# A cross-attention and RWKV block on one core: the beginning reordered, and the key and query stacks stored and loaded in other pieces

## The chip, the core and the metric

The kernel runs on one core of a Trainium2 chip. Its engines are TensorE (PE), VectorE (DVE), ScalarE (ACT), GpSimd (POOL) and SyncE (SP), which here only issues DMAs. The metric is the time of one execution on the device in microseconds; several runs give a median, and one further execution was profiled.

## The reference

Eight sequences (B = 8) of 256 tokens with 256 channels attend to a context of 1601 rows each, and the result goes through a second block.

```python
q, k, v = x @ Wq + bq, ctx @ Wk + bk, ctx @ Wv + bv      # 32 query heads, 8 key heads, 8 digits each
scores  = einsum('bkgld,bksd->bkgls', q, k) / sqrt(8) + mask
x = layernorm(softmax(scores) @ v @ Wo + bo + x) * gamma + beta
# second block, channels in 32 heads of 8, with a state of 8 x 8 per head:
xk, xw, xv, xr, xg = token-shift mixes of layernorm(x)
s = k v^T + w * s;  out = r (u k v^T + s)                # scan over the 256 tokens
x = x + (groupnorm(out) * silu(g)) @ Wo.T;  then a gated feed-forward
```

## The kernel before, in words

The program is written out by hand for five engines, with semaphores between them. It is a pipeline over turns (`it`, 0 to 9). In turn `it` element b = it is scored and weighed, a = it + 1 is split and stacked, f = it + 2 is projected, c = it - 1 goes through the output projection and the second block's scan, and d = it - 2 through its feed-forward. A turn has 52 steps; in each TensorE scores two tiles, ScalarE exponentiates them, TensorE weighs the values with them, and the other work is put between at fixed steps.

**Precision by parts.** Keys and queries are float32 values split into three bf16 parts (high, middle, low), and the products of the parts that matter are added within one matmul by stacking them: 6 pairs of parts (`Q_PARTS`, `K_PARTS`) x 8 digits = 48 partitions (`DOT`), for two key heads at partitions 0 to 47 and 64 to 111. So each element has stacks `k_stack[g]`, `q_stack[g]` for g = 0, 1, each with four key heads. Partitions 32 to 63 and 96 to 127 are first cleared (lines 1495, 1496): 1.0 for keys, 0 for queries. Three partitions above the 48 take the row shift.

**From parts to stacks.** The parts leave SBUF for DRAM and return as stacks. `store_k_parts` (line 321) writes each of the six key slots (parts 0, 0, 0, 1, 1, 2) as a DMA of its own (64 partitions x 1601 bf16) into `k_stacked`, laid out as [element, key head, slot, digit, 1601]. `store_q_parts` (line 326) writes six slots x two channel halves, 12 DMAs, into `q_stacked` [element, head, slot, digit, 256]. `load_stacks` (line 332) waits for both and reads a stack by two DMAs for keys (48 partitions x 2 heads x 1601) and two for queries (48 x 8 heads x 256). All of them are SP's, in SP's program order, in every turn: stack 1 of b at step 0, right ahead of the residual rows `x_rows` of c (line 359), both stores of a at step 8, the spread of the values (line 364) at step 18, the next context at step 20, stack 0 of a at step 26.

**POOL's order in a turn** (line 577 on): copy the values, add `bo` to `x_rows` once they have landed (`add_bo`, 528), split queries and keys of a (`split_q`, `split_k`, 507, 496), then the roots for the layer norms of c (`root`, 520). VectorE's layer norm (1359 to 1373) waits for the root, and VectorE's row maxima of stack 1 (`reduce_step`) stand behind it.

**The beginning** runs once. SP loads w_kv, b_kv, w_q, chan and ident (456 to 460, one semaphore `early_in` for all five), the context in four pieces and x_t. VectorE clears both stack pairs and a few borders and `vs` (1493 to 1499). TensorE waits for `early_in` and `cleared`, writes a product of zeros over the accumulator `po`, then projects (`first_projection`, 1053): four pieces of keys and values into banks 7, 5, 7, 5, each reuse waiting for ScalarE's bias, and the queries into bank 6. ScalarE (`project`, 628) adds the bias and makes the high and middle parts, VectorE (1314 to 1323) the rests and low parts, each over all 1601 keys. SP loads the mask, waits for the parts, stores 6 + 12, loads stack 0. VectorE looks at the mask (`see_mask`) while it waits. Then four rounds on the first 128 keys give the row maxima, the shift is turned, split, sent through DRAM onto the stack (`shift_to_dram`, `shift_to_stack`), and turn 0 begins. SP loads the context of element 1 only after `mask_seen`, because the mask lies in the context's buffer. POOL issues 46 late loads of weights (line 617) once the last piece of the context is there.

```python
for r, n in enumerate(K_PARTS):                                                    # 323
    sp.dma_start(k_st_d[a % B][:, r], k_parts[:, n, :]).then_inc(k_out.sem, 16)
sp.dma_start(k_stack[g][p0:p0 + DOT, :, :],                                        # 340
             k_st_d[n % B][k0:k0 + 2].rearrange("k r d s -> (r d) k s"))
```

## Time and profile before

| What | Before |
|---|---|
| median of 3 runs | 1243.32 us (1239.51 to 1243.42) |
| the profiled execution, its own time | 1244.15 us |
| its span, first to last instruction | 1242.3 us |
| mean granted TensorE clock | 0.942 |
| busy: PE, DVE, ACT, POOL | 85%, 50%, 70%, 25% |
| first context piece issued, last | 3.18 us, 4.7 us |
| first score tile of turn 0 | 76.35 us |
| DMA written to DRAM, read | 18.62 MB, 50.74 MB |

A DMA row of a view gives the mean busy share of the core's 16 DMA engines in tenths, slice by slice, and the row under it GB/s. A timeline row may hold several instructions of one kind (x8); its length is from the first's start to the last's end. In square brackets stands how long the engine was idle before, and what released it. The profile names buffers without their numbers. All matmuls stand under line 710, a helper's.

### The profile page before, as it was taken

To read this page: it belongs to the slowest core of one execution; us is meant where nothing else is said; L and a number is where in the kernel's file an instruction comes from. 1 tells how busy PE (TensorE), PEld (TensorE's weight loads), DVE (VectorE), ACT (ScalarE), POOL (GpSimd) and SP (SyncE) were. 2 spreads that over 40 slices of the span, in tenths; PEclk is the share of its full clock that TensorE was granted. 3 is DMA by queue.
4 is the path that set the end of the run, shared out by engine and by line. 5 is a ranking of instruction groups with operands and counts; after the bars stand their busy time and mean duration, and the time that the engine had idled before them with its cause. 6 is when DMAs were issued, how large, how long until landed. Compare 5 with 4: busy or idle time off the path is not lost.

```text
span 1242.3 us, 18191 instructions
## 1 busy us (share of the span) xinstructions
PE 1050.1 (85%) x7100; PEld 374.4 (30%) x7100; DVE 615.0 (50%) x1113; ACT 870.0 (70%) x953; POOL 305.6 (25%) x349
## 2 busy tenths in 40 slices
PE   3058998899999998999999999999998899986663
PEld 1012222232334233333333233323332233313312
DVE  5324122575375645484367536564547334735463
ACT  1037988688877887778877887888777877884010
POOL 6204104140232305230414023220523001401140
PEclk9569999999999999999999999999999899999766
DMA  5643413271227123441337122803252022300310
GB/s 174 160 96 120 95 55 66 55 151 55 42 75 142 24 75 94 63 103 55 74 65 141 55 46 72 149 16 88 82 69 35 2 42 31 57 1 1 51 26 11
DMA packets 65565, 87.47 MB, mean 70 GB/s; under 512 B 8208, under 2 KB 48192, under 8 KB 65472
## 3 DMA queue, kind: packets, MB, share of 16 engines
q1 hardware_dynamic: 63536, 82.91, 31.2%
q0 software_dynamic: 1936, 3.32, 0.9%
q8 instruction: 58, 0.95, 0.3%
q14 instruction: 35, 0.29, 0.1%
HBM read 50.74 MB, written 18.62 MB: 56 GB/s over the span
## 4 chain that ended last, share of the span: by engine, by line
PE 35%; issue 20%; DVE 14%; ACT 13%; POOL 8%; DMA 6%; SPq 3%; POOLq 0%; DVEq 0%; ACTq 0%
PE psum L710 35%; ACT probs L649 10%; DMA vs<-v_c 5%; DVE row_max L1162 3%; DVE vs L1282 2%; SPq L371 2%; POOL k_rest L501 1%; POOL k_parts L505 1%; DVE vs L1275 1%; POOL xm L536 1%; DVE k_stack L1495 1%; POOL vs L553 1%; ACT L649 1%; ACT L686 1%; DVE xa L1249 1%
## 5 line engine op out<-in xcount | busy, mean ns | idle before, releaser
L649 ACT ACTIVATE probs<-psum 128x1024 f32<-128x1024 f32 (+1 forms) x832 | 800.5, 1022 | 244.5 <-PE psum L710 243.5
L710 PE MATMUL psum<-probs,v_aug 128*9 128x512 f32 (+1 forms) x3328 | 423.8, 608 | 0.1
L710 PE MATMUL psum<-q_stack,k_stack 64*128 64x512 bf16 (+1 forms) x1664 | 291.5, 391 | 54.4 <-ACT probs L649 43.3
L710 PEld LDWEIGHTS psum<-q_stack,k_stack 64*128 64x128 bf16 (+1 forms) x1664 | 71.2, 95 | 425.6 <-ACT probs L649 350.4
L1282 DVE TENSOR_TENSOR_SCAN vs<-w_c,vs 128x514 f32<-128x514 f32 x64 | 101.8, 1591 | 21.7 <-POOL vs L544 19.9
L710 PEld LDWEIGHTS psum<-probs,v_aug 128*9 128x9 f32 (+1 forms) x3328 | 62.1, 90 | 161.9 <-issue 148.1
L553 POOL TENSOR_TENSOR vs<-r_c,vs 128x512 f32<-128x512 f32 x64 | 86.1, 1354 | 100.3 <-DVE tmp L1421 59.6
L1162 DVE TENSOR_REDUCE row_max<-psum 128x8 f32<-128x1024 f32 x64 | 78.0, 1219 | 46.3 <-PE psum L710 45.8
L536 POOL TENSOR_TENSOR xm<-tmp,xa 128x512 f32<-128x512 f32 x40 | 45.6, 1156 | 206.3 <-DVE tmp L1269 206.3
L523 POOL TENSOR_TENSOR rstd<-moments,eps 128x2 f32<-128x2 f32 x24 | 4.7, 194 | 302.4 <-DVE moments L1235 302.4
L1209 DVE COPY o_raw<-psum 128x512 f32<-128x512 f32 x32 | 22.1, 692 | 98.6 <-PE psum L710 98.6
L710 PE MATMUL psum<-k_stack,q_stack 48*128 48x128 bf16 x512 | 26.8, 225 | 48.2 <-DMA q_stack<-q_stacked 29.5
L1269 DVE SCALAR_TENSOR_TENSOR tmp<-psum,chan,sx 128x256 f32<-128x256 f32 x80 | 33.4, 473 | 49.8 <-PE psum L710 49.8
L710 PE MATMUL psum<-ctx_t,w_kv 128*128 128x400 f32 (+1 forms) x128 | 49.5, 521 | 6.7 <-DVE attn L1223 6.0
L488 POOL COPY v_aug<-v_st 128x384 f32<-128x384 f32 x16 | 8.1, 505 | 161.7 <-PE psum L710 160.0
L1275 DVE TENSOR_TENSOR vs<-k_c,vs 128x512 f32<-128x512 f32 x64 | 47.0, 735 | 0.3
L710 PEld LDWEIGHTS psum<-k_stack,q_stack 48*128 48x128 bf16 x512 | 18.4, 97 | 65.9 <-issue 54.7
L1140 DVE TENSOR_SCALAR kv<-psum,b_kv 128x400 f32<-128x400 f32 (+1 forms) x28 | 17.6, 630 | 39.4 <-PE psum L710 39.4
L710 PEld LDWEIGHTS psum<-ctx_t,w_kv 128*128 128x128 f32 x128 | 23.0, 192 | 26.2 <-DVE attn L1223 8.5
L1469 DVE RECIPROCAL xm<-xm 128x512 f32<-128x512 f32 x8 | 26.8, 3348 | 7.1 <-ACT xm L686 7.1
L1157 DVE TENSOR_REDUCE mask_max<-ctx_t 128x1 f32<-128x1601 f32 x16 | 28.8, 1810 | 0.0
L1131 DVE TENSOR_SCALAR q<-psum,chan 128x256 f32<-128x256 f32 x16 | 7.0, 480 | 39.4 <-PE psum L710 23.8
(175 smaller groups left out, 1062.7 us busy)
## 6 DMA issues: line engine op xcount, KB each, us to landing
vs<-v_c SPq DMA_DIRECT2D x64, 257.0 KB, 7.4
ctx_t<-in_mask SPq DMA_DIRECT2D x8, 1601.0 KB, 6.5
k_stacked<-k_parts SPq DMA_DIRECT2D x48, 200.1 KB
k_stack<-k_stacked SPq DMA_DIRECT2D x32, 300.2 KB, 6.7
ctx_t<-in_ctx_t SPq DMA_DIRECT2D x24, 400.0 KB, 5.9
q_stacked<-q_parts SPq DMA_DIRECT2D x96, 64.0 KB, 2.0
q_stack<-q_stacked SPq DMA_DIRECT2D x32, 192.0 KB, 7.3
ctx_t<-in_ctx_t SPq DMA_DIRECT2D x8, 401.0 KB, 6.3
```

The costliest lines, as they stand in the source:

```text
L371: sp.dma_start(vs[:, j, :, :].rearrange("p e l -> p (e l)"), src.broadcast_to([16, HD, EC * (L + 1)]))\
L536: nc.gpsimd.tensor_tensor(xm[MIX_ORDER[n]][:, :, :], tmp[n % 2][:, :, :], xa[:, :, 1:L + 1], ALU.add)\
L553: nc.gpsimd.tensor_tensor(vs[:, j, :, 0:L], r_c[:, :, :], vs[:, j, :, 0:L], ALU.mult)\
L649: nc.scalar.activation(probs[turn_step % NP][t][0:w, :, :], ps[t][0:w, :, :], ACT.Exp).then_inc(exped.sem, 1)
L710: return nc.tensor.matmul(dst, lhsT, rhs, start=start, stop=stop)
L1157: nc.vector.tensor_reduce(mask_max[:, a, lc:lc + 1], ctx_t[:, lc, :], AX.X, ALU.max, apply_absolute_value=True).then_inc(mask_seen.sem, 1)
L1162: nc.vector.tensor_reduce(row_max[:, 8 * r:8 * r + 8], psum[:, 6:8, :].rearrange("p a (u k) -> p (a u) k", k=P), AX.X, ALU.max)\
L1209: nc.vector.tensor_copy(o_raw[:, :], po).then_inc(o_kept.sem, 1)
L1269: last = nc.vector.scalar_tensor_tensor(tmp[n % 2][:, e, :], halves(at)[:, e, :], vec(f"s{f}", e), sx[:, e, :], ALU.add, ALU.mult)
L1275: nc.vector.tensor_tensor(vs[:, j, :, 1:L + 1], k_c[:, :, :], vs[:, j, :, 1:L + 1], ALU.mult)\
L1282: nc.vector.tensor_tensor_scan(flat, w_c[:, :, :].rearrange("p e l -> p (e l)"), flat, 0.0, ALU.mult, ALU.add)\
L1469: link(nc.vector.reciprocal(std_o[:, :, :], std_o[:, :, :]))
```

## The change

VectorE clears stack pair 0 and POOL pair 1. The loads of w_q, chan and ident are issued behind the context, with a semaphore of their own. The first projection uses banks 0 to 3, and TensorE waits for the clearing only behind it. The split of element 0's keys goes by halves of 801 and 800, interleaved with the biases, and ScalarE runs one small Exp at the start. ScalarE's queue stores element 0's queries and loads half of its first stack. The mask's load and its look come after the stack loads and after the shift's split. In all turns: keys are stored by three DMAs (the source repeated 3, 2, 1 times) into a layout with the slot outside the key head, queries by six DMAs of the three distinct parts, and a stack is loaded by ten DMAs (each half: two for keys, three for queries) instead of four. POOL's late loads come in another order and behind its clearing. POOL's own waits of the key split (`split_turn`) count without the first turn.

```diff
+RUNS = [(0, 3), (3, 2), (5, 1)]
...
+SPLIT = [(0, 801), (801, 800)]
...
-KV_FIRST = (7, 5, 7, 5)
+KV_FIRST = (0, 1, 2, 3)
...
-        k_st_d = nc.dram_tensor("k_stacked", [B, KV, NR, HD, S], BF16).ap()
-        q_st_d = nc.dram_tensor("q_stacked", [B, NH, NR, HD, L], BF16).ap()
+        k_st_d = nc.dram_tensor("k_stacked", [B, NR, KV, HD, S], BF16).ap()
+        q_st_d = nc.dram_tensor("q_stacked", [B, NH, 3, HD, L], BF16).ap()
...
-        early_in, late_in = sig("early_in", 16 * 5), sig("late_in")
-        cleared, prepared, acc_cleared, v_ones = sig("cleared"), sig("prepared"), sig("acc_cleared"), sig("v_ones")
+        early_in, early_q, late_in = sig("early_in", 16 * 2), sig("early_q", 16 * 3), sig("late_in")
+        cleared, cleared_up = sig("cleared"), sig("cleared_up")
+        prepared, acc_cleared, v_ones, warmed = sig("prepared"), sig("acc_cleared"), sig("v_ones"), sig("warmed")
...
+        k_out, q_out = sig("k_out", 16 * len(RUNS)), sig("q_out", 16 * 3 * EC)
...
+        def split_turn(a):
+            return a - 1 - a // B
+        def load_stack_half(eng, n, g, half):
+            k0, p0 = 4 * g + 2 * half, HALF * half
+            for t in range(2):
+                eng.dma_start(k_stack[g][p0:p0 + DOT, t, :], k_st_d[n % B, :, k0 + t])\
+                  .then_inc(stack_in[g].sem, 16)
+            for r0, m in RUNS:
+                lo, hi = p0 + HD * r0, p0 + HD * (r0 + m)
+                eng.dma_start(q_stack[g][lo:hi, :, :, :].rearrange("p t h l -> p (t h) l"),
+                              q_st_d[n % B][4 * k0:4 * k0 + 8, 0:m].rearrange("h r d l -> (r d) h l"))\
+                  .then_inc(stack_in[g].sem, 16)
+        def store_queries(eng, a):
+            for m in range(3):
+                for c in range(EC):
+                    eng.dma_start(q_st_d[a % B][16 * c:16 * c + 16, m], q_parts[:, m, c, :]).then_inc(q_out.sem, 16)
...
-                for r, n in enumerate(K_PARTS):
-                    sp.dma_start(k_st_d[a % B][:, r], k_parts[:, n, :]).then_inc(k_out.sem, 16)
+                for r0, m in RUNS:
+                    src = k_parts[:, K_PARTS[r0], :].rearrange("p (a s) -> p a s", a=1)
+                    sp.dma_start(k_st_d[a % B, r0:r0 + m].rearrange("r k d s -> (k d) r s"), src.broadcast_to([64, m, S]))\
+                      .then_inc(k_out.sem, 16)
             def store_q_parts(a):
                 sp.wait_ge(q_low.sem, q_low.at(a))
-                for r, n in enumerate(Q_PARTS):
-                    for c in range(EC):
-                        sp.dma_start(q_st_d[a % B][16 * c:16 * c + 16, r], q_parts[:, n, c, :]).then_inc(q_out.sem, 16)
-
-            def load_stacks(n, g):
+                store_queries(sp, a)
+            def load_stacks(n, g, halves=(0, 1)):
                 if n > 0:
                     sp.wait_ge(scored.sem, scored.at(n - 1, TILES // GQ * (g + 1)))
                     sp.wait_ge(sub_reduced[g].sem, sub_reduced[g].at(n - 1))
                 sp.wait_ge(k_out.sem, k_out.at(n))
                 sp.wait_ge(q_out.sem, q_out.at(n))
-                for half in range(2):
-                    k0, p0 = 4 * g + 2 * half, HALF * half
-                    sp.dma_start(k_stack[g][p0:p0 + DOT, :, :],
-                                 k_st_d[n % B][k0:k0 + 2].rearrange("k r d s -> (r d) k s")).then_inc(stack_in[g].sem, 16)
-                    sp.dma_start(q_stack[g][p0:p0 + DOT, :, :, :].rearrange("p t h l -> p (t h) l"),
-                                 q_st_d[n % B][4 * k0:4 * k0 + 8].rearrange("h r d l -> (r d) h l"))\
-                      .then_inc(stack_in[g].sem, 16)
+                for half in halves:
+                    load_stack_half(sp, n, g, half)
...
                 if not general:
-                    load_mask(lo)
+                    sp.dma_start(w_q[:, :, :], dram["L0_xattn_Wq"].rearrange("(c p) n -> p c n", p=P))\
+                      .then_inc(early_q.sem, 16)
+                    sp.dma_start(chan[:, :, :], dram["chan"]).then_inc(early_q.sem, 16)
+                    sp.dma_start(ident[:, :], dram["ident"]).then_inc(early_q.sem, 16)
                     sp.wait_ge(cleared.sem, 1)
+                    sp.wait_ge(cleared_up.sem, 1)
                 store_k_parts(lo)
-                store_q_parts(lo)
-                load_stacks(lo, 0)
+                load_stacks(lo, 0, (0,))
                 if general:
                     full_masks(lo, 0)
+                else:
+                    load_mask(lo)
...
+            pool.wait_ge(v_ones.sem, 1)
+            link(nc.gpsimd.memset(k_stack[1][32:64, :, :], 1.0))
+            link(nc.gpsimd.memset(q_stack[1][32:64, :, :, :], 0.0))
+            link(nc.gpsimd.memset(k_stack[1][96:128, :, :], 1.0))
+            nc.gpsimd.memset(q_stack[1][96:128, :, :, :], 0.0).then_inc(cleared_up.sem, 1)
+            pool.wait_ge(cleared_up.sem, 1)
             pool.wait_ge(ctx_in[NK - 1].sem, ctx_in[NK - 1].at(0))
...
             def project(a):
+                turn = a // B
                 act.wait_ge(early_in.sem, early_in.at(0))
-                for n, (at, w) in enumerate(PIECE):
+                def biased(n):
+                    at, w = PIECE[n]
                     act.wait_ge(kv_proj.sem, kv_proj.at(a, n + 1))
                     nc.scalar.activation(kv32[:, at:at + w], bank(KV_FIRST[n])[:, 0:w], ACT.Identity, bias=b_kv[:, 0:1])\
                       .then_inc(kv_biased.sem, 1)
-                act.wait_ge(kv_biased.sem, kv_biased.at(a))
-                nc.scalar.activation(k_parts[:, 0, :], kv32[0:64, :], ACT.Copy).then_inc(k_high.sem, 1)
+                def high(h):
+                    at, w = SPLIT[h]
+                    act.wait_ge(kv_biased.sem, kv_biased.at(a, 2 * h + 2))
+                    nc.scalar.activation(k_parts[:, 0, at:at + w], kv32[0:64, at:at + w], ACT.Copy).then_inc(first_high.sem, 1)
+                def mid(h):
+                    at, w = SPLIT[h]
+                    act.wait_ge(first_r1.sem, first_r1.at(turn, h + 1))
+                    nc.scalar.activation(k_parts[:, 1, at:at + w], k_rest[:, at:at + w], ACT.Copy).then_inc(first_mid.sem, 1)
+                biased(0)
+                biased(1)
+                high(0)
+                biased(2)
+                mid(0)
+                biased(3)
+                high(1)
+                mid(1)
                 act.wait_ge(q_scaled.sem, q_scaled.at(a))
                 nc.scalar.activation(q_parts[:, 0, :, :], q32[:, :, :], ACT.Copy).then_inc(q_high.sem, 1)
-                act.wait_ge(k_r1.sem, k_r1.at(a))
-                nc.scalar.activation(k_parts[:, 1, :], k_rest[:, :], ACT.Copy).then_inc(k_mid.sem, 1)
                 act.wait_ge(q_r1.sem, q_r1.at(a))
                 nc.scalar.activation(q_parts[:, 1, :, :], q_rest[:, :, :], ACT.Copy).then_inc(q_mid.sem, 1)
+                act.wait_ge(q_low.sem, q_low.at(a))
+                store_queries(act, a)
+                act.wait_ge(cleared.sem, 1)
+                act.wait_ge(k_out.sem, k_out.at(a))
+                act.wait_ge(q_out.sem, q_out.at(a))
+                load_stack_half(act, a, 0, 1)
...
+            nc.scalar.activation(partial_max[:, 0, 0:1], ones[:, :], ACT.Exp).then_inc(warmed.sem, 1)
...
             def first_projection(a, general):
                 for n in range(NK):
-                    if n >= 2:
-                        pe.wait_ge(kv_biased.sem, kv_biased.at(a, n - 1))
                     project_kv(a, n, KV_FIRST[n])
+                pe.wait_ge(early_q.sem, early_q.at(0))
                 project_q(a, 6)
+                if a == 0:
+                    pe.wait_ge(cleared.sem, 1)
+                    zeros = vs[:, 0:2, :, :].rearrange("p j e l -> p (j e l)")
+                    mm(po, zeros[:, 0:P], zeros[:, P:P + 512]).then_inc(acc_cleared.sem, 1)
...
+                def rest(h):
+                    at, w = SPLIT[h]
+                    dve.wait_ge(first_high.sem, first_high.at(lo // B, h + 1))
+                    nc.vector.tensor_tensor(k_rest[:, at:at + w], kv32[0:64, at:at + w], k_parts[:, 0, at:at + w],
+                                            ALU.subtract).then_inc(first_r1.sem, 1)
+                def low(h):
+                    at, w = SPLIT[h]
+                    dve.wait_ge(first_mid.sem, first_mid.at(lo // B, h + 1))
+                    return nc.vector.tensor_tensor(k_parts[:, 2, at:at + w], k_rest[:, at:at + w], k_parts[:, 1, at:at + w],
+                                                   ALU.subtract)
+                rest(0)
+                low(0)
+                rest(1)
                 scale_q(lo, 6)
-                dve.wait_ge(k_high.sem, k_high.at(lo))
-                nc.vector.tensor_tensor(k_rest[:, :], kv32[0:64, :], k_parts[:, 0, :], ALU.subtract).then_inc(k_r1.sem, 1)
+                low(1).then_inc(k_low.sem, 1)
                 dve.wait_ge(q_high.sem, q_high.at(lo))
                 nc.vector.tensor_tensor(q_rest[:, :, :], q32[:, :, :], q_parts[:, 0, :, :], ALU.subtract).then_inc(q_r1.sem, 1)
-                dve.wait_ge(k_mid.sem, k_mid.at(lo))
-                nc.vector.tensor_tensor(k_parts[:, 2, :], k_rest[:, :], k_parts[:, 1, :], ALU.subtract).then_inc(k_low.sem, 1)
                 dve.wait_ge(q_mid.sem, q_mid.at(lo))
                 nc.vector.tensor_tensor(q_parts[:, 2, :, :], q_rest[:, :, :], q_parts[:, 1, :, :], ALU.subtract)\
                   .then_inc(q_low.sem, 1)
                 keep_v(lo, 0, 5)
                 keep_v(lo, 1, 7)
-                if not general:
-                    see_mask(lo, 0)
-                    see_mask(lo, 1)
                 for r in range(4):
                     reduce_step(lo, 0, r, general)
                 negate_shift(lo, 0)
                 split_shift(lo, 0)
+                if not general:
+                    see_mask(lo, 0)
+                    see_mask(lo, 1)
...
-            for g in range(GQ):
-                for p0 in (32, 96):
-                    nc.vector.memset(k_stack[g][p0:p0 + 32, :, :], 1.0)
-                    nc.vector.memset(q_stack[g][p0:p0 + 32, :, :, :], 0.0)
+            for p0 in (32, 96):
+                nc.vector.memset(k_stack[0][p0:p0 + 32, :, :], 1.0)
+                nc.vector.memset(q_stack[0][p0:p0 + 32, :, :, :], 0.0)
```

Moved in `late_loads`: w_o, the rows, maa_w1, the five square weights, Wv and Wg come first, then heads, heads_turned, maa_w2, td_w1 and td_w2; the rest as before. SP's three early loads stand behind `load_x_t` now.

## Rows read from the trace of the kernel before

**Rows 1.** The page: span, granted clock in 40 slices, the mask's reductions.

```profile
span 1242.3 us, 18191 instructions
...
PEclk9569999999999999999999999999999899999766
...
L1157 DVE TENSOR_REDUCE mask_max<-ctx_t 128x1 f32<-128x1601 f32 x16 | 28.8, 1810 | 0.0
```

**Rows 2.** The chain that ended last, first 80 us: start, length (us), what.

```profile
1.46 2.73 DVE k_stack L1495
...
5.96 2.73 DVE k_stack L1495
...
20.07 4.03 PE psum L710 x6
...
35.13 1.83 DVE k_parts L1320
...
50.85 2.03 DMA q_stacked<-q_parts
...
54.32 6.71 DMA q_stack<-q_stacked
...
76.35 0.63 PE psum L710 x2
```

**Rows 3.** Waits of the whole span: us in total, times, longest.

```profile
POOL x_rows L531 <- DMA x_rows<-in_x: 31.2, 7, 5.4
```

**Rows 4.** Timeline of turn 1, by engine: start, length (us), engine, line, operation.

```profile
195.24 0.47 SPq L362 DMA_DIRECT2D x_rows<-in_x  x1
...
202.92 1.27 POOL L531 TENSOR_TENSOR x_rows<-x_rows,rows 128x512 f32<-128x512 f32 x1 [5.43 <-DMA x_rows<-in_x]
...
218.41 0.74 DVE L1242 TENSOR_SCALAR x<-x,moments,rstd 128x256 f32<-128x256 f32 x2 [8.47 <-POOL rstd L526]
...
225.30 0.40 PE L710 MATMUL psum<-k_stack,q_stack 48*128 48x128 bf16 x8 [0.65 <-DVE row_max L1162]
```

**Rows 5.** Timeline of the beginning, and one POOL cast of turn 1.

```profile
11.40 0.80 POOL L617 DMA_DIRECT2D heads<-in_heads  x1 [10.21 <-DMA ctx_t<-in_ctx_t]
...
21.91 3.52 PE L710 MATMUL psum<-ctx_t,w_kv 128*128 128x401 f32 x8
...
25.48 1.08 ACT L632 ACTIVATE kv<-psum,b_kv 128x401 f32<-128x401 f32 x2
...
29.75 1.54 ACT L635 ACTIVATE k_parts<-kv 64x1601 bf16<-64x1601 f32 x1
...
30.93 0.88 DVE L1131 TENSOR_SCALAR q<-psum,chan 128x256 f32<-128x256 f32 x2 [10.97 <-PE psum L710]
...
33.46 0.67 DVE L1318 TENSOR_TENSOR q_rest<-q,q_parts 128x512 f32<-128x512 f32 x1
...
207.85 1.51 POOL L499 CAST k_parts<-kv 64x1601 bf16<-64x1601 f32 x1
```

**Rows 6.** DMA issues from 0 to 14 us: count, KB each, median us to landing.

```profile
ctx_t<-in_ctx_t SPq DMA_DIRECT2D x3, 400.0 KB, 5.9
ctx_t<-in_ctx_t SPq DMA_DIRECT2D x1, 401.0 KB, 4.7
```

**Rows 7.** DMA share (tenths) and rate, 350 to 360 us, 40 slices: key stores.

```profile
DMA  0000000345338555545545545445544469965432
GB/s 0 0 0 0 0 0 0 77 102 102 64 77 270 205 192 192 205 179 179 179 179 192 167 154 167 141 192 192 179 167 192 167 244 376 376 239 159 147 116 103
```

**Rows 8.** The same, 136 to 150 us: the four loads of stack 0.

```profile
DMA  0000092899999998999999920000000000000000
GB/s 0 0 0 0 0 137 55 338 318 123 133 117 147 192 176 171 227 155 105 116 110 129 138 31 10 0 0 0 0 0 0 0 0 0 0 0 0 0 0 0
```

**Rows 9.** Timeline of turn 2: stack 0 issued, stack 0 first read.

```profile
397.97 0.47 SPq L340 DMA_DIRECT2D k_stack<-k_stacked  x1
...
414.02 0.39 PE L710 MATMUL psum<-k_stack,q_stack 48*128 48x128 bf16 x8
```

More of the change, by code:

```diff
@@ L222, in build @@
         mask_seen = sig("mask_seen", LC)
-        stack_in = [sig(f"stack_in{g}", 64) for g in range(GQ)]
+        stack_in = [sig(f"stack_in{g}", 16 * 2 * (2 + len(RUNS))) for g in range(GQ)]
         sub_scored = [sig(f"sub_scored{g}", 4) for g in range(GQ)]
@@ L273, in late_loads @@
             c = dram
-            yield heads[:, :], c["heads"]
-            for m in range(HD):
-                yield heads_turned[16 * m:16 * m + 16, :], c["ident"][0:16, 0:16]
             yield w_o[:, :, :], c["L0_xattn_Wo"].rearrange("(c p) n -> p c n", p=P)
@@ L1499, in _ @@
             nc.vector.memset(vs[:, 0:2, :, :], 0.0).then_inc(cleared.sem, 1)
-            dve.wait_ge(early_in.sem, early_in.at(0))
+            dve.wait_ge(early_q.sem, early_q.at(0))
             all_turns(0, False)
```

25 lines of the change are left out of this document (11 added, 14 removed).

## The prediction

> **What bounds the kernel now.** I read the page first, then the chain that ended last in order of time, the timeline of the first 80 us, the DMA view of three stretches, and the waits. The page gives a span of 1242.3 us; the granted clock stands at 9 tenths or nearly so in the first slice of 31 us, at 5 and 6 in the next two, and at 9 or more through the body of the loop [rows 1]. Ahead of them lies a serial beginning. Its chain [rows 2] runs: VectorE clears the two pairs of stacks from 1.46 on, TensorE starts only at 20.07, the three-way split of the keys ends at 36.96, SP issues 18 stores of which the last begins at 50.85 and has landed at 52.88, four stack loads land by 61.03, four rounds of row maxima and the shift follow, and the first score tile stands at 76.35. Nothing of the loop runs before that, so what the beginning loses in length the whole kernel loses, as long as the loop is untouched. But the change touches the loop too, because the layout of the two DRAM tensors is shared by all turns. There a second chain matters. In each turn POOL waits for the residual rows, which SP issues right behind the four loads of stack 1; seven of eight times it waited, 31.2 us in all [rows 3]. In turn 1 the rows are issued at 195.24, POOL adds the bias at 202.92, runs the two splits behind it in order, and VectorE has idled 8.47 us when the root lets it go at 218.41; TensorE's round at 225.30 waited for VectorE's maximum [rows 4]. So a later landing of these rows lengthens a turn one for one.
>
> **The change, part by part, the beginning.** *Clearing.* The stack blocks cost VectorE 2.73 us each, and with the queries' block and the gaps they start 4.5 apart, four times [rows 2]. Two of the four go to POOL, so VectorE is done at about 11.0 instead of 20.0, and TensorE no longer waits for it before projecting (it waits before its clearing product, behind the queries). POOL's casts give 1.51 us for 1601 elements [rows 5], so about 3 us for 3202 and 1 to 2 for the queries' block, twice: done by 9.5 to 11.5. As an upper bound, a POOL operation with two inputs takes 1.27 for 512 elements [rows 4], which would make it about 22 to 27; SP's first store waits for it, and from 17.5 on it would be the path. I take 11.
>
> *Projection.* It now starts with the first piece of the context. The pieces landed 4.7 and 5.9 us after their issue [rows 6], the first issued at 3.2; three loads (w_q, chan, ident) go behind them, which moves their issue up by 1.5 us, to 1.7. So piece 0 is there at about 6.2 and piece 3 at about 9.3. Eight instructions took 3.52 us, 0.44 each, straight after 20 us of idling [rows 5]; the clock of the first slice, which holds them, is near full [rows 1], so the engine had the 2.4 GHz level after idling from the start, and I take it here too. Four pieces of four make 7.0 us, less a little as the later ones run faster, so the last is done at about 12.6. With four banks TensorE doesn't wait for ScalarE. The table load moves under this wait; the first bias at 25.48 came 1.3 us late for it [rows 5]. At the 1.2 GHz level the four pieces would take up to twice as long, and the projection would end 6 us later.
>
> *Split by halves.* After the last piece: one bias (0.54, half of 1.08), behind ScalarE's middle cast of half 0, then half of a cast (1.54), a subtraction (1.83), a cast and a subtraction [rows 2, 5], with the queries' scaling of 0.88 beside the second cast, 0.1 of it showing. That is 0.5 + 0.5 + 3.4 + 0.1 + 0.3 of handovers = 4.8, so the low part is ready at 17.4 instead of 36.96.
>
> *Stores.* Keys: three issues instead of six. The old ones run at half of the DMA engines: while only they run, the share stands at 4 to 5 tenths and 170 to 205 GB/s [rows 7]. Their DRAM side has an outermost count of 8 (the heads), and the new one has 64 (heads and digits merge), so I expect all 16 engines: 1.2 MB at some 340 GB/s, 3.6 us. Queries: six issues on ScalarE's queue instead of twelve on SP's. Three more steps of some 0.67 bring their low part to 19.6. The first 17 issues of now took 0.82 each (36.96 to 50.85) [rows 2]; at that the sixth begins at 23.7 and has landed 2.03 later, at 25.7. POOL's late loads started at 11.40 [rows 5] and start at the same time now, the big weights first (2.6 MB), so the stores share the engines with them. I add 0.8: both are out at 26.5 (25 to 29), against 52.88.
>
> *Stack loads.* This is the disputed part. Ten loads in place of four, the same bytes: 615 KB of keys and 393 KB of queries. The old ones took 6.5 us with all 16 engines at 9 tenths, the first keys at 318 to 338 GB/s, which would make 1.8 us of keys and leave 4.7 for queries, whose stretches run at 105 to 147 [rows 8]. Their DRAM side begins with a merged count of 48. The new key loads can't merge part and digit, because the heads lie between them: the DRAM side begins with 6. If the outermost count sets the number of engines, as 8 did in [rows 7], six engines carry all keys at 24 GB/s each, 144 together: 4.3 us. The same six also carry 64 query packets each instead of 48 (leading counts 24, 16 and 8 on 12, 16 and 8 engines). If memory limits those packets, the other ten engines have done theirs meanwhile and 2.3 us are left, in all 6.6: 0.1 more than now. If each engine's own rate limits them, 4.7 x 64/48 = 6.3, in all 10.6: 4.1 more. I take 2.0 more, the middle, and call this d. The Trainium skill, DMA: Bandwidth & Descriptors, section "Why a DMA increments its semaphore by 16 and not by 1", says that the outermost counts of both sides set it, by the largest number up to 16 that divides both. By it the key loads run on 6 engines; the share of 5 tenths with a count of 8 agrees. First load: 8.15 from the last store's landing to the last load's [rows 2] becomes 10.15, so the stacks are in at 36.65 against 61.03.
>
> Behind this nothing moves: rounds, shift and its detour take 15.3 as before, 61.03 to 76.35. The mask is loaded behind the stacks, 1.6 MB or some 5 us of transfer, under the rounds. Its two reductions of 1.81 [rows 1] come behind the shift's split, beside the shift's way through DRAM; the next context waits for them, and I set 0.4 for what shows. Gain of the beginning: 24.4 - 0.4 = 24.0.
>
> **The loop.** SP's nine stores fewer and twelve loads more nearly cancel in issue time, and at the stores SP is waiting anyway. Stack 0 is issued at 397.97 and first read at 414.02, 16 us later [rows 9]; 6 more issues and d fit in that. What doesn't fit is the load of stack 1, with the residual rows behind it: they are spread over all engines and land when the slowest is through, so d later. Turns 1 to 6 have the splits on POOL behind this wait and pay 6 x 2.0 = 12; turn 7 has no split and turn 0 no such rows. The sum: 24.0 - 12 = 12.0 less, 1244.15 - 12.0 = 1232.15 on the profiled execution's own time, which stands 0.8 above the median of 1243.32; so 1231 for the median. In general the difference is -26.0 + 7d, one d in the beginning and six in the loop.
>
> **Rivals.** *The engines are all used.* The loads may still spread over 16 engines; then d is 0 and only the beginning changes: 1243.3 - 26.0 = 1217. For it: the destination still has 48 partitions. Against: the key stores at half share, with 64 partitions on their SBUF side. *The loads cost more than they save.* With engine-bound packets, uneven queues or keys below 24 GB/s per engine, d is 4.5: -26.0 + 31.5 = +5.5, 1249. It decides from d = 3.7 on. For it: in [rows 8] the second key load ran at 171 to 227, not at 338, beside query packets. Against: with six engines reading, each meets less traffic. *The beginning gives less.* POOL's clearing or the late loads hold the stores: 5 to 8 us less of it, 1236 to 1239.
>
> **Numbers.** Forecast 0.47, all engines 0.25, less at the beginning 0.10, dearer loads 0.18. Some 0.3% (3.7 us) is what a measurement of this kernel can tell from no change. The forecast's own d runs from 1 to 3, 1224 to 1238, and with a beginning 2 us shorter or longer than reckoned 1222 to 1240. By case: the forecast is faster but for 0.02 within the bound; all engines is faster; of the lesser beginning 0.06 is faster and 0.04 within; of the dearer loads 0.05 is within and 0.13 slower. Faster 0.45 + 0.25 + 0.06 = 0.76, the same 0.11, slower 0.13. The range runs from 1214 to 1247.
>
> **What would show it.** First projection near 6 us, key split ready near 17.4, stacks in near 37, first score near 52. In the DMA view the key stores at 9 tenths, the stack loads at 9 tenths first and then at 3 to 5; POOL's wait for the residual rows at 6.5 us a turn instead of 4.5. It is wrong if the loads keep a share of 9 and take 6.5 us (then nearer 1217), or if POOL's wait passes 8 us (then slower than before), or if the keys' split starts only after 20.

## The result, and the profile after

The changed kernel takes 1247.97 us (median of 20 runs) beside 1243.59 for the kernel before on the same chip (20 runs): a ratio of 1.0033 with a 95% interval of 1.0019 to 1.0047. It is slightly slower, where 1231 and faster was forecast, and lies just outside the forecast's range of 1214 to 1247. One run of each kernel took far longer (1389.71 and 2466.13 us); the ratio goes by the others. Its profiled execution took 1242.88 us, near the low end of its runs (1240.69 upwards), so its rows show some 5 us less than its typical run costs.

The page of the changed kernel, against [rows 1]:

```profile
span 1241.1 us, 18221 instructions
...
PEclk8589998999999999999999999999999999999666
...
L1211 DVE TENSOR_REDUCE mask_max<-ctx_t 128x1 f32<-128x1601 f32 x16 | 28.8, 1810 | 0.0
```

The body is granted 9 tenths as before, so at this resolution the clock doesn't tell the two apart (a small difference in the loop is taken up below), and the mask's two reductions last 1.81 each as before. The chain that ended last, first 64 us (start, length, what), against [rows 2]; L290 are the query stores, L279 and L283 the stack loads:

```profile
5.35 4.54 PE psum L764 x8
...
16.75 0.99 DVE k_parts L1377
...
19.03 0.70 DVE q_parts L1388
19.75 0.63 ACTq L290
...
20.42 2.36 ACTq L290
22.81 2.48 ACTq L290
...
27.63 3.92 DMA q_stacked<-q_parts
...
35.18 12.68 DMA q_stack<-q_stacked
...
48.13 0.62 PE psum L764 x8
...
63.24 0.63 PE psum L764 x2
```

Up to 19.75 everything stands where the forecast had it. Then the last query store lands at 31.55 instead of 26.5, and the stacks are in at 47.86 instead of 36.65: 16.3 us after the stores, where it had been 8.15. The first score stands at 63.24: 13.1 earlier than at 76.35, not 24.

SP's timeline of the same stretch shows what was issued right behind SP's half of the stack loads, while these still ran; the mask is 1.6 MB:

```profile
17.84 3.27 SPq L350 DMA_DIRECT2D k_stacked<-k_parts  x3
31.61 1.71 SPq L279 DMA_DIRECT2D k_stack<-k_stacked  x2
33.36 1.71 SPq L283 DMA_DIRECT2D q_stack<-q_stacked  x3
35.12 0.41 SPq L343 DMA_DIRECT2D ctx_t<-in_mask  x1
```

In the loop, the waits of the whole span (us in total, times, longest), against [rows 3]:

```profile
POOL x_rows L553 <- DMA x_rows<-in_x: 49.6, 7, 7.9
DVE x L1296 <- POOL rstd L548: 42.0, 8, 10.9
```

POOL waits 7.1 us a turn for the residual rows instead of 4.5. What this costs I read from the copy that begins each turn on POOL, v_aug with 65x32; here those of turns 1 and 7:

```profile
181.94 0.21 POOL L514 COPY v_aug<-v_st 65x32 f32<-65x32 f32 x1
...
1001.56 0.21 POOL L514 COPY v_aug<-v_st 65x32 f32<-65x32 f32 x1
```

The six turns between them last 819.6 us. In the kernel before they stood at 197.28 and 1004.01, 806.7. The loop gives back 12.9 of the 13.1. Of the rest, turn 0 is 2.2 shorter (118.7 from the first score to turn 1's copy, where it was 120.9) and what follows turn 7's copy 1.3 longer: the profiled span is 1.2 us below that of the kernel before.

The DMA view (share in tenths and GB/s in 40 slices) of the stack-0 load in turn 0's second half, 121 to 135 us, against [rows 8]:

```profile
DMA  0000022325885233466854445432110000000000
GB/s 0 0 0 0 0 18 37 91 91 164 225 184 84 55 73 109 119 158 184 255 135 167 138 152 146 82 71 60 58 37 25 10 0 0 0 0 0 0 0 0
```

and of the key stores, 341 to 351 us, against [rows 7]:

```profile
DMA  0300000009999999999999999999999993996000
GB/s 0 66 0 0 0 0 0 0 0 231 218 205 192 205 205 205 205 205 205 205 192 205 205 205 205 205 205 205 192 218 205 205 192 107 340 373 226 4 0 0
```

The loads spread thin: shares mostly of 2 to 6, two slices at 8, and a tail at 1 to 3, about 9 us long, where four loads had held 9 tenths for 6.5. The stores did get all engines, as forecast, and moved no faster for it: 6.2 us for 1.2 MB, where 340 GB/s and 3.6 us were reckoned.

### The profile page after: what moved, and what is told of

The parts are those of the page before. It is cut to its first block, busy times and chain, and to the rows that moved or that the text cites. A ratio compares the mean times of both kernels' runs of the same rounds, so it can differ in the third digit from the quotient of the medians.

```text
span 1241.1 us, 18221 instructions
## 1 busy us (share of the span) xinstructions
PE 1051.0 (85%) x7100; PEld 375.7 (30%) x7100; DVE 608.2 (49%) x1111; ACT 870.4 (70%) x956; POOL 314.3 (25%) x353
## 4 chain that ended last, share of the span: by engine, by line
PE 28%; issue 24%; DVE 14%; ACT 12%; POOL 11%; DMA 7%; SPq 2%; ACTq 1%; POOLq 0%; DVEq 0%
PE psum L764 28%; ACT probs L702 9%; DMA vs<-v_c 5%; DVE row_max L1216 3%; DVE vs L1336 2%; SPq L391 2%; POOL k_rest L523 2%; POOL k_parts L527 1%; DVE vs L1329 1%; DMA q_stack<-q_stacked 1%; POOL xm L558 1%; POOL vs L575 1%; POOL rstd L548 1%; POOL k_parts L525 1%; ACT L702 1%
## 5 line engine op out<-in xcount | busy, mean ns | idle before, releaser
L1296 DVE TENSOR_SCALAR x<-x,moments,rstd 128x256 f32<-128x256 f32 x16 | 5.9, 411 | 42.0 <-POOL rstd L548 42.0
```

## The experiments

All are timed in five rounds beside the kernel before, whose median there was 1243.8 to 1245.8. "Wait" is POOL's wait for the residual rows; "six turns" is the time between the two copies above; "stacks" runs from the last query store's landing to the last stack load's. One profiled execution gives each of these.

### Loop: is it the stores and loads, and are they late for the rows?

Four runs. **b_newio** is the kernel before with the change's layouts, stores and loads in all turns, all on SP. **a_oldloop** is the changed kernel with those forms for element 0 alone and the old ones (in DRAM tensors of their own) for elements 1 to 7. **a_xfirst** and **b_xfirst** are the two kernels with SP's order at step 0 turned round:

```
-                            if b is not None:
-                                load_stacks(b, 1)
                             if c is not None:
                                 load_x_rows(c)
+                            if b is not None:
+                                load_stacks(b, 1)
```

> The kernel before, with the new layout, stores (3 + 6) and loads (10 per stack) in all turns, all issued by SP; the beginning is otherwise the old one. If the new loads are what the loop lost, six turns of 2.2 us and the first load a few us longer: 13 to 20 us slower than before, 1257 to 1264, and POOL's wait for the residual rows near 50 us in all. If the loss came with the new beginning instead (clock, phase of the turns), within 3 us of before, and the wait near 31.

> The kernel after, with the new layout, stores and loads for element 0 alone; elements 1 to 7 use tensors of the old layout with the old 18 stores and four loads. Loads theory: the beginning keeps its 13 us and the loop gives nothing back, 1228 to 1234, POOL's wait near 31 us. Rival (the loop lost its time for another reason): 1243 to 1248.

> The kernel after, with SP issuing the residual rows ahead of the loads of stack 1 instead of behind them; the loads stay as they are. If what costs is that the rows queue behind the loads, POOL's wait goes to nearly zero, and the time to 1226 to 1234. If the loads cost in another place (stack 0 late for its rounds, the other DMAs), the wait goes but the time stays above 1240.

> The kernel before with the residual rows first. POOL's wait of 31 us goes; the chain through POOL's splits is the critical one in about every turn by small amounts, so 3 to 10 us faster, 1233 to 1240. If TensorE is just as late by its own work, no change.

| run | median us | ratio [95%] | wait, us | six turns | first score |
|---|---|---|---|---|---|
| before | 1243.59 | | 31.2 | 806.7 | 76.35 |
| after | 1247.97 | 1.0033 [1.0019, 1.0047] | 49.6 | 819.6 | 63.24 |
| b_newio | 1259.63 | 1.0116 [1.0088, 1.0145] | 52.3 | 827.6 | 74.63 |
| a_oldloop | 1227.81 | 0.9881 [0.9853, 0.9908] | 29.9 | 804.7 | 61.96 |
| a_xfirst | 1221.07 | 0.9803 [0.9769, 0.9838] | none | 796.7 | 63.00 |
| b_xfirst | 1237.83 | 0.9936 [0.9910, 0.9961] | none | 796.9 | 76.84 |

The new forms alone make the kernel before 1.2% slower; without them in the loop the change gains 1.2%. With the rows issued first the wait is gone in both kernels and their six turns agree within 0.2 us. So the whole loss of the loop hangs on this one wait: stack 0's loads have 16 us to spare [rows 9], the rows behind stack 1's have none. a_xfirst came out below its range of 1226 to 1234, because the new order takes away not only what the loop had lost but also the wait that the kernel before had (six turns 806.7, then 796.9).

### Loop: six engines, or six more issues?

The rows are issued behind ten loads instead of four. Either the engines are late, or SP is. **b_ten** keeps the old layout and stores of the kernel before, but has ten loads that all begin with a merged count of 48:

```
-  k_stack[g][p0:p0 + DOT, :, :] <- k_st_d[n % B][k0:k0 + 2] "k r d s -> (r d) k s"
+  for t: k_stack[g][p0:p0 + DOT, t, :] <- k_st_d[n % B][k0 + t] "r d s -> (r d) s"
-  q_stack (t h) l <- q_st_d[n % B][4 * k0:4 * k0 + 8] "h r d l -> (r d) h l"
+  the same for heads 0 to 3, 3 to 6 and 6 to 8
```

**b_pad** is b_ten with one row of padding behind each part, so that part and digit can't merge; loads, bytes and stores stay:

```
-        k_st_d = nc.dram_tensor("k_stacked", [B, KV, NR, HD, S], BF16).ap()
+        k_st_d = nc.dram_tensor("k_stacked", [B, KV, NR, HD + 1, S], BF16).ap()
```

**b_newk** and **b_newq** are the kernel before with the change's key or query forms alone. In the expectations below the merged count is given as 96 and a part as sixteen rows. A part has eight rows of digits, so it is 48 rows a load, 48 merged and 6 not, and the padding is a ninth row; 48 is a multiple of 16 too, so what the runs test stays the same.

> The kernel before with its own DRAM layouts and its own 18 stores, but with ten loads per stack in place of four: the keys by t, the queries in three pieces of 3, 3 and 2 heads, so that every load still begins with a count of 96 and can use all 16 engines. Theory of the engines (the loads of the change are late because few engines carry them): the residual rows land as before, POOL's wait for them stays near 31 us (4.5 a turn) or a little over, the time at the kernel before's, 1241 to 1247. Rival, the count of issues (SP issues six more DMAs at about 0.55 us each before the residual rows, so these start 3.3 us later, on whatever engines the loads are): the wait is 48 to 54 us as with the change's loads, and the time 1255 to 1262.

> The run b_ten with one thing more: the keys' DRAM tensor holds a seventeenth row behind each part's sixteen, which is never written or read, so that part and digit no longer merge and each key load begins with a count of 6 instead of 96. Stores, bytes, number of loads and their order are those of b_ten, and so is the rest of the layout. Theory of the engines (it is the outer count that makes the change's key loads late): POOL's wait for the residual rows goes from 28.7 us to 44 to 52, and the time from b_ten's 1240 to 1254 to 1260. Rival (it is the head between part and digit, that is where the rows lie in DRAM, or the three broadcast key stores): the wait stays at 28 to 33 and the time at 1239 to 1243.

> The kernel before with the change's key layout alone: three key stores, and two key loads of 96 rows for each half, which have six as their outer count; six loads per stack in all. Theory of the engines: the keys are 0.6 of a stack's bytes and sit on 6 engines, so most of the lateness is here: POOL's wait 42 to 48 us, time 1250 to 1256. Rival, the count of issues: two issues more per stack, 1.1 us a turn, wait 37 to 40, time 1246 to 1250.

> The kernel before with the change's query layout alone: six query stores, and three query loads for each half on 12, 16 and 8 engines at most; eight loads per stack in all. Theory of the engines: little lateness from the queries alone, wait 33 to 38, time 1243 to 1248. Rival, the count of issues: four issues more per stack, 2.2 us a turn, wait 43 to 47, time 1250 to 1255. The query stores are six instead of twelve, and the last of them is the key stores' predecessor, so the beginning may be some 3 us shorter in both theories.

| run | loads per stack, keys' outer count | median us | ratio [95%] | wait, us | six turns |
|---|---|---|---|---|---|
| b_ten | 10, 48 | 1240.29 | 0.9974 [0.9962, 0.9986] | 28.7 | 803.5 |
| b_pad | 10, 6 | 1257.06 | 1.0094 [1.0071, 1.0117] | 48.2 | 819.2 |
| b_newk | 6, 6 | 1257.26 | 1.0112 [1.0087, 1.0136] | 45.1 | 818.3 |
| b_newq | 8, 48 | 1239.68 | 0.9970 [0.9954, 0.9985] | 33.8 | 807.0 |

Six more issues cost nothing; b_ten is even a little faster than the kernel before. The outer count of the keys alone costs 16.8 us between the medians; the two ran on different chips, and by their ratios to the kernel before it is 1.2%, some 15 us. b_newq's gain is made in the beginning, where six query stores fewer bring its first score to 73.01; its loop is as long as before. SP's timeline and the DMA view of turn 2's stack-1 load, first of b_ten (slices of 0.275 us, 326 to 337):

```profile
326.31 0.79 SPq L341 DMA_DIRECT2D k_stack<-k_stacked  x2
327.15 1.38 SPq L345 DMA_DIRECT2D q_stack<-q_stacked  x3
328.57 0.89 SPq L341 DMA_DIRECT2D k_stack<-k_stacked  x2
329.51 1.39 SPq L345 DMA_DIRECT2D q_stack<-q_stacked  x3
330.95 0.43 SPq L365 DMA_DIRECT2D x_rows<-in_x  x1
```

```profile
DMA  0000759999999998999779999999994000000000
```

and of b_pad, where the loads begin at 332.29 (332 to 343):

```profile
332.29 1.57 SPq L341 DMA_DIRECT2D k_stack<-k_stacked  x2
333.90 1.40 SPq L345 DMA_DIRECT2D q_stack<-q_stacked  x3
335.34 1.48 SPq L341 DMA_DIRECT2D k_stack<-k_stacked  x2
336.86 1.41 SPq L345 DMA_DIRECT2D q_stack<-q_stacked  x3
338.32 0.43 SPq L365 DMA_DIRECT2D x_rows<-in_x  x1
```

```profile
DMA  0000007500368964343344779465989954543110
```

b_ten holds 7 to 9 tenths for 7 us and is through, the rows with it. b_pad swings between 3 and 9 tenths and needs 9 us. Issuing key loads with the small outer count is itself dearer (1.5 us for two instead of 0.8), so the rows are issued 6.0 us after the first load instead of 4.6. Over the seven turns POOL starts on the rows 9.0 us after the first load's issue in b_ten and 11.8 in b_pad; of these 2.8 more, 1.3 lie before the rows' issue and 1.5 behind it. Issue time alone doesn't make the rows late: the kernel before issues them 1.8 us after the first load and b_ten 5.2, and POOL starts at 9.3 and 9.0. The Trainium skill, DMA: Bandwidth & Descriptors, section "Why a DMA increments its semaphore by 16 and not by 1", has a DMA use the largest number of engines up to 16 that divides both outermost counts; a load of 48 rows with 6 outermost on its DRAM side would run on six. The views agree: six of sixteen busy would be 4 tenths at most, and b_pad's share falls to 3 and 4 where b_ten's stays at 7 and more. Which engines carried what was not read out.

The key forms cost more over the runs than in the profile of the changed kernel. Of the profiles shown here and below, the seven that load keys by 6 and have the rows behind them give six turns of 818.3 to 827.6 us, 822.7 in the mean; the six with the rows behind them and keys by 48 give 803.5 to 807.7, mean 805.8. That is 16.9, or 2.8 a turn; the changed kernel's profiled 12.9 is at the low end, which goes with its time at the low end of its runs.

Part of that price lies in the clock. Over the six turns TensorE is granted 0.97 or 0.98 in each of the seven and 0.99 in each of the six, and its matmuls are busy for 751 to 758 us instead of 746 to 749, 6.4 more in the mean, of the 16.9. With the rows first it is 0.99 and 747.5 even with the change's loads (a_xfirst), so the lower clock comes with the wait. How much of the 6.4 adds to the time, and how much lies beside the wait, the runs don't separate.

### The beginning: late loads, mask, queue, keys

Each of these is the changed kernel with one edit. **a_late**: POOL issues its late loads once stack 0 is in. **a_mask**: the mask waits for stack 0. **a_spq**: SP issues the query stores behind the key stores. **a_oldk**: the keys' old layout, six stores and one load per half in all turns. **a_oldkmask**: a_oldk and a_mask.

```
a_late   pool, behind copy_v(lo, 0):  + pool.wait_ge(stack_in[0].sem, stack_in[0].at(0)), then the late loads
a_mask   sp, ahead of load_mask(lo):  + sp.wait_ge(stack_in[0].sem, stack_in[0].at(lo))
a_spq    act: - store_queries(act, a)     sp, behind store_k_parts(lo): + store_q_parts(lo)
a_oldk   k_st_d [B, KV, NR, HD, S]; stores and key loads as in the kernel before
```

> The changed kernel with POOL's 50 or so late loads (3.3 MB) issued only once stack 0 has landed, instead of from 10.85 us on. Theory of the contention (query stores and first stack loads are slow because the late loads fill the same 16 engines): the last query store lands near 27 instead of 31.55, the stack loads take 12 instead of 16.3 from there, and the first score stands at 54 to 58 instead of 63.2; time 1239 to 1243. Rival, the issuing and the few engines alone make it slow: the first score stays at 61 to 64 and the time within 2 us of the changed kernel's 1248.

> The changed kernel with the mask's load (1.6 MB) issued only once stack 0 has landed. Theory that the mask shares engines with the first stack load: the stacks take 13 to 15 us from the last query store instead of 16.3, the first score stands 1 to 3 us earlier, 60 to 62; the time 1244 to 1248, less what the later mask costs the next context's load. Rival, the stacks are limited by the six engines of the keys, which the mask hardly loads more than the others: first score within 0.7 us of 63.2, time unchanged at 1246 to 1250.

> The changed kernel with the six query stores issued by SP behind the key stores instead of by ScalarE. If issuing from ScalarE's queue itself is dear (1.4 us each there), SP issues them at 0.6 to 0.8 from 21 on, they have landed by 28 instead of 31.55, and the first score is 2 to 4 us earlier, time 1244 to 1247. Rival, each issue waits because the engines' queues are full with late loads and key stores, on whatever queue it is issued: SP takes 1.2 to 1.5 us for each too, they land at 31 to 33, and the first score is within 1.5 us of 63.2 or later; time 1247 to 1250.

> The changed kernel with the keys' DRAM layout, six stores and one load per half of the kernel before, everything else of the change kept (queries' new layout, both queues, clearing, halves, banks). Theory of the keys (all that the loop loses is the key loads, whose outer count is 6; the query forms lose nothing): POOL's wait for the residual rows goes back to 32 to 36 us, the six turns to 803 to 808, and the time is 1227 to 1233. In the beginning three more stores of keys cost issue time on SP beside ScalarE's, and the key loads are quicker: the first score at 60 to 64. Rival, the query loads on 12, 16 and 8 engines carry a good part of it once the beginning is short: wait 40 or more, time 1237 or more.

> The run a_oldk with the mask's load issued once stack 0 has landed. Theory that the mask was dear only because its packets stand in line on the six engines that carry the change's keys: with the keys on all engines moving it gives little, the stacks take 7 to 9 us from the last query store instead of 9.1 and the first score stands at 55 to 57 instead of 56.65; time 1222 to 1226. Rival, the mask costs the first stack load by its bytes whatever the keys' engines, as it did with 5.8 us in the changed kernel: stacks in 3.5 to 4, first score at 51 to 53, time 1219 to 1222.

| run | median us | ratio [95%] | first query issue, last landed | stacks, us | first score | wait, us |
|---|---|---|---|---|---|---|
| after | 1247.97 | 1.0033 [1.0019, 1.0047] | 19.75, 31.55 | 16.3 | 63.24 | 49.6 |
| a_late | 1242.04 | 0.9991 [0.9974, 1.0009] | 20.85, 29.2 | 13.0 | 59.12 | 52.3 |
| a_mask | 1241.46 | 0.9981 [0.9962, 1.0000] | 20.94, 31.2 | 10.5 | 56.90 | 50.9 |
| a_spq | 1246.83 | 1.0025 [1.0007, 1.0043] | 20.56, 32.0 | 13.5 | 60.87 | 51.3 |
| a_oldk | 1225.05 | 0.9839 [0.9812, 0.9866] | 19.70, 32.4 | 9.1 | 56.65 | 34.3 |
| a_oldkmask | 1223.40 | 0.9830 [0.9808, 0.9853] | 20.69, 33.2 | 8.3 | 56.67 | 32.2 |

*The mask and the keys.* Moving the mask takes 5.8 us from the stacks and 6.5 from the time, far more than I expected of it. Giving the keys their 16 engines back, with the mask left where it was, takes 7.2. Doing both takes 8.0. So the mask is dear only together with the six-engine keys: with the keys on all engines it costs 0.8. The chain of a_mask:

```profile
27.95 3.25 DMA q_stacked<-q_parts
...
34.64 7.09 DMA q_stack<-q_stacked
...
56.90 0.63 PE psum L765 x2
```

and the DMA view from 31 to 49 us, first of the changed kernel, then of a_mask:

```profile
DMA  0411253535888899999989999999993433422000
```

```profile
DMA  0312533367899794434441000092899999994000
```

In a_mask the stack loads stand without the mask (POOL's last small late loads are issued up to 36.4) and end in slices of 4 tenths; the mask follows behind the gap at 9 tenths. In the changed kernel the mask fills all 16 engines at once and the tail of 3 to 4 tenths comes behind it, at 45 to 48 us. I read that as the few engines that carry the keys having the mask's packets to move too; the 2 x 2 of the runs shows the coupling, the order within an engine's queue was not looked at. a_oldk also came below its range (1225.05, where 1227 to 1233 was expected; first score 56.65 for 60 to 64): I hadn't counted the first stack load's gain.

*The queue.* a_spq's six issues took 20.56 to 28.5, 1.3 us each, like ScalarE's 1.4. So the queue is not what makes them dear, and the rival stands. What does is to be seen in b_newk, whose late loads are all issued by 36.5; its first three query issues, right behind the key stores, are

```profile
40.61 2.01 SPq L333
42.66 1.01 SPq L333
43.72 0.60 SPq L333
```

and all later ones take 0.60. Key stores just issued make the next issues dear, without any late load. a_spq's stacks came 2.8 sooner all the same, for which I have no reason beyond the spread of one profile.

*The late loads.* Without them (a_late) the stores took 8.3 us from first issue to landing instead of 11.8, and the stacks 13.0 instead of 16.3. But they moved into the way of the shift's detour, 7.5 us instead of 6.3. The first score gained 4.1 where I expected 5 to 9, the time 5.9.

*a_oldk* answers the main question: undoing the keys' part alone turns the change from 0.3% slower into 1.6% faster, by the loop (six turns 807.7) and the first stack load.

### Together

**a_best** is a_oldkmask with the rows first and the late loads behind stack 0; **a_best2** has the late loads behind the shift; **a_best3** has them where the changed kernel has them; **a_oldkx** has only a_oldk and the rows first.

> Together what the runs so far name: the changed kernel with the keys' old layout, stores and loads, the residual rows issued ahead of stack 1, and POOL's late loads and the mask issued once stack 0 is in. If the parts add: the changed kernel with the rows first stands at 1221, the late loads give 4 to 6 and the mask up to 1, the key forms nothing while the rows go first: 1214 to 1218, first score near 57, no wait of POOL for the rows. Rival, with keys back on 16 engines stack 1 too is in earlier and gives some more: 1208 to 1213; or the late loads collide with the shift's detour and turn 0: 1219 to 1223.

> The run a_best with POOL's late loads issued only once the shift's digits are in stack 0 as well. Theory that in a_best the late loads were moved out of the stores' way into that of the shift's detour, which took 10.8 us there instead of 6.1: first score at 52 to 53.5 instead of 57.2, time 1208 to 1212. Rival, late loads so late hold up POOL's splits of element 1 and stack 1's load in turn 0, which gives the gain back: 1213 to 1218.

> The run a_best with POOL's late loads where the changed kernel has them, from 10.85 us on. What the late loads cost the query stores is then read against a_best2 with nothing else different: the stores land at 31.5 instead of 29.8 or less, the stacks are in near 39, the first score stands at 53.5 to 55; time 1210 to 1214. Rival, the late loads cost the stores nothing and they are late by the key stores alone: first score within 0.5 us of a_best2's.

> The changed kernel with only two things undone or moved: the keys' old layout, stores and loads (a_oldk), and the residual rows issued ahead of stack 1 (a_xfirst); mask and late loads stay where the change has them. In a_mask and a_oldkmask turn 0 took 121 us from the first score to turn 1's first projection of v, with the mask in its place (after, a_oldk) 118.7. If the later mask costs turn 0 what it saved ahead of it, this kernel is as fast as the three fuller versions, 1212 to 1216, with the first score at 56 to 58 and turn 1 near 175. Rival, the mask's place matters once the keys are on 16 engines: 1217 to 1221.

| run | median us | ratio [95%] | first query issue, last landed | stacks, us | first score | turn 1 at |
|---|---|---|---|---|---|---|
| a_best | 1214.45 | 0.9743 [0.9715, 0.9772] | 20.78, 29.7 | 7.4 | 57.23 | 178.3 |
| a_best2 | 1213.68 | 0.9745 [0.9721, 0.9769] | 20.80, 30.1 | 7.4 | 52.74 | 177.3 |
| a_best3 | 1215.29 | 0.9758 [0.9734, 0.9781] | 20.40, 31.8 | 8.6 | 55.72 | 176.9 |
| a_oldkx | 1210.81 | 0.9725 [0.9695, 0.9755] | 20.96, 32.9 | 9.4 | 57.64 | 177.0 |

a_best2 against a_best3 prices the late loads: 2.1 us at the stores, 1.2 at the stacks, 3.0 at the first score. With them, the mask and the keys out of the way the first score stands at 52.74, where the forecast had 52:

```profile
20.80 0.62 ACTq L289
...
26.57 3.49 DMA q_stacked<-q_parts
...
31.62 5.84 DMA q_stack<-q_stacked
...
52.74 0.62 PE psum L763 x2
```

But nothing of this reaches the time. Turn 1 begins within 1.5 us in all four, and the intervals overlap; the simplest is at least as good as the others. Turn 0 takes 124.6 us from the first score in a_best2 and 119.4 in a_oldkx. Most of these 5 us can be seen in the traces. SP loads the mask of element 1 at 71.03 in a_best2, while POOL's late loads are still going out and the DMA share is at 9 tenths; it lands 12.4 us later, and VectorE waits for it with stack 1's row maxima behind:

```profile
DVE mask_max L1210 <- DMA ctx_t<-in_mask: 2.8, 1, 2.8
```

In a_oldkx the mask is issued later, at 75.55, but has the engines to itself and lands in 6.7 us; VectorE doesn't wait for it, and TensorE goes on behind the first of these maxima at 89.89, where it does at 88.30 in a_best2. So of 4.9 us gained at the first score 1.6 are left there; the rest goes before turn 1. That was a_best2's rival (1213 to 1218), which came true. What wins is the pair of edits in a_oldkx: 2.75% faster than the kernel before, 3% faster than the change as it was made. In its waits the residual rows no longer appear, and the root behind them has fallen from 42.0 to

```profile
DVE x L1293 <- POOL rstd L545: 11.2, 8, 3.0
```

## Why the prediction was wrong

**Right: the beginning up to the stores.** VectorE's clearing done at 11.0 (10.96), POOL's blocks 2.76 and 1.80 us each and done at 10.5 (9.5 to 11.5), first projection near 6 (5.35), last at 12.6 (12.5), keys' low part at 17.4 (17.74), queries' at 19.6 (19.73). The clock was at its 2.4 GHz level there, with 1.00 granted from 5 to 17 us. Halves, banks and divided clearing bring what was reckoned.

**Right: the loop's mechanism, sign and size.** "What doesn't fit is the load of stack 1, with the residual rows behind it" is what all loop runs say: 12 us forecast, 12.9 in the profiled execution. Over the runs it is nearer 17, so d = 2.0 should have been 2.8 there. Part of that is the clock at 0.97 to 0.98 instead of 0.99, for which the sum had no term. The share of 3 to 5 tenths on the loads and POOL's wait above 6.5 us a turn (7.1) came as said. The rival that all engines are used is out: b_pad and b_ten differ in the outer count alone and stand 15 to 17 us apart.

**Near, though it looked wrong: d of the first load.** With the mask out of the way the load takes 10.5 us (a_mask) where 8.15 + 2.0 = 10.15 was forecast. Since the last small late loads still ran beside it, the closeness of the two is partly luck.

**Wrong: the mask at nothing.** The step reads "The mask is loaded behind the stacks, 1.6 MB or some 5 us of transfer, under the rounds". It was placed under the rounds in the sum, but it is issued at 35.12, right behind SP's half of the loads, with 12.7 us of them still to come. It cost 5.8 us, and 0.8 with the keys on all engines (a_oldk, a_oldkmask), so it was dear because of the keys' form. I had reckoned both facts, the few engines and the mask behind, and never put them together: the load that sat on six engines was the one that its neighbour on all sixteen hurt.

**Wrong: both stores out at 26.5.** They were out at 31.55, past the forecast's own 25 to 29. The sixth query issue began at 27.63 instead of 23.7 and had landed 3.92 later instead of 2.03. The issue price of 0.82 was a mean of 17 issues of the kernel before: up to 1.4 amid the key stores, 0.60 for the last nine, behind them. The six of the change fall wholly into the dear stretch and took 1.3 to 1.4, on either queue. And the key stores, reckoned at 340 GB/s and 3.6 us, move 205 even on all engines (6.2 us in the loop), so this stretch is longer too. The 0.8 added for the late loads was 2.1 (a_best3 less a_best2) to 3.5 (after less a_late). The rest, 9.3 us in a_best2 where 6.1 was reckoned without late loads, stands beside the key stores, which b_newk's issues name as the cause of the price; how much of the landing is theirs was not tested alone.

Put in numbers: 24.4 us less 5.0 for the stores and 6.1 for the stacks leaves 13.3, and 13.1 was measured. Less the loop's 12.9 in the profiled execution, that is no change; less 17, the mean that the other profiles give, slower by 4, and the medians differ by 4.4. The case that came true was none of the rivals alone: "the beginning gives less" named the late loads and had 5 to 8 us, it gave 11, and it came together with a dearer loop. The two were treated as excluding each other, though both draw on the same engines.

## What to carry to other kernels

Ask of every DMA in a rewritten layout what its outermost counts still merge to, not how many DMAs there are: three key stores fewer brought the last store's landing only from 52.88 to 51.52 (b_newk), and key loads with six outermost cost some 17 us in six turns. Here a transfer on few engines was hurt far more by a large load beside it than one on all engines, so its price must be taken with its neighbours. And look first at what is queued behind the slow transfer on its queue: issuing the small load that someone waits for ahead of the large ones with time to spare gained 0.6% in the kernel before and 2.2% in the changed one, and made both blind to the loads' form. Take the price of an issue from issues in the same surroundings, not from a mean over a long row of them.

## What was not expected of the hardware

The key stores on all engines (9 tenths) move 205 GB/s; the old ones at 4 to 5 tenths moved 141 to 205, mostly 167 to 205 [rows 7]. Twice the engines gave no more bytes a second, so here the engine count was not what bound them.

Issuing two key loads with six outermost held SP for 1.57 us, with 48 outermost for 0.79 (b_pad, b_ten), at the same bytes and rows.

b_ten, with six loads more per stack, is 0.26% faster than the kernel before, outside its interval. Its wait is 28.7 us instead of 31.2 and its six turns 803.5 instead of 806.7; finer loads seem to let the residual rows through a little sooner. This was not followed up.
